# Five gather passes of a graph network get a bound on the index, and the ring of rows is cleared once

## The reference, cut to what matters

```python
edge_index = jnp.stack([src, dst])
h = relu(layernorm(x)); x = x + L0(h)  # attention: q[src] . k[dst], softmax over dst, sum of v[src]
h = relu(layernorm(x)); x = x + L1(h)  # gated unit: mean of h[src] by dst, and mean of h[dst] by src
h = relu(layernorm(x)); x = x + L2(h)  # relations: sum of hW[edge_type, src] by dst, over the degree
h = relu(layernorm(x)); x = x + L3(h)  # attention with LeakyReLU scores, softmax over dst, batch norm
```

## Time and profile before

| what | value |
|---|---|
| time, median of three | 8359.04 us (8329.57 to 8359.52) |
| span of the profiled execution, first to last instruction | 7751.3 us |
| the profiled execution's own time | not recorded; the median lies 607.7 us above the span |
| PE busy | 6251.2 us (81%) |
| DVE busy | 4997.1 us (64%) |
| POOL busy | 4545.2 us (59%) |
| ACT busy | 1562.8 us (20%) |
| mean granted TensorE clock | 0.822 |
| DMA, software queue (POOL's) | 242400 packets, 709.04 MB |
| DMA, hardware queue (SP's) | 187350 packets, 275.48 MB |

### The profile page before, as it was taken

The page is one execution under the profiler, slowest core; times in us unless marked ns, Lnnn a source line. Parts: engine busy times, 40 slices in busy tenths (PEclk is TensorE's granted clock), DMA queues, the critical chain, the costliest instruction groups (busy, mean ns, idle before and its releaser), DMA issues. The chain is left out here.

```text
span 7751.3 us, 82773 instructions
## 1 busy us (share of the span) xinstructions
PE 6251.2 (81%) x23966; PEld 3661.9 (47%) x23966; DVE 4997.1 (64%) x11031; ACT 1562.8 (20%) x3423; POOL 4545.2 (59%) x4618
## 2 busy tenths in 40 slices
PE   8699999996477777888888899888888778878783
PEld 4366666664233333444444444433333355555552
DVE  7799999998666666444444444444444577777777
ACT  5222222222000000000000255200000133333331
POOL 1155555553677777777777311377777356666660
PEclk9799999998765666798988899855555789999997
DMA  2266666666433333544444544433333544444453
GB/s 91 75 177 177 177 176 177 176 177 166 122 99 97 97 98 99 116 132 131 132 128 132 136 164 164 140 101 102 101 101 101 127 130 115 116 115 116 117 107 101
DMA packets 430184, 989.81 MB, mean 128 GB/s; under 512 B 120243, under 2 KB 203377, under 8 KB 423094
## 3 DMA queue, kind: packets, MB, share of 16 engines
q0 software_dynamic: 242400, 709.04, 34.6%
q1 hardware_dynamic: 187350, 275.48, 10.8%
HBM read 851.94 MB, written 132.00 MB: 127 GB/s over the span
## 5 line engine op out<-in xcount | busy, mean ns | idle before, releaser
L876 PE MATMUL psum<-rows,oh 128*128 128x257 f32 (+1 forms) x5280 | 2444.9, 577 | 657.0 <-DMA rows<-h_tab,src_i 201.9
L876 PEld LDWEIGHTS psum<-rows,oh 128*128 128x128 f32 x5280 | 1172.6, 264 | 1879.0 <-issue 1092.2
L885 DVE TENSOR_TENSOR acc<-acc,psum 128x257 f32 (+1 forms) x1760 | 741.4, 421 | 1110.6 <-PE psum L876 986.1
L799 POOL DMA_INDIRECT rows<-qv_tab,src_i x880 | 845.9, 961 | 848.5 <-PE psum L1060 496.5
L1395 POOL DMA_INDIRECT rows<-xh_tab,src_i x880 | 874.2, 993 | 562.3 <-PE psum L1474 248.6
L818 POOL DMA_INDIRECT rows<-h_tab,src_i x880 | 911.3, 1036 | 290.8 <-issue 244.3
L818 POOL DMA_INDIRECT rows<-hw_tab,rel_i x880 | 875.4, 995 | 283.7 <-issue 267.7
L818 POOL DMA_INDIRECT rows<-h_tab,wts x880 | 875.8, 995 | 268.0 <-issue 247.3
L885 DVE TENSOR_TENSOR kh<-kh,psum 128x257 f32 x880 | 370.8, 421 | 643.2 <-PE psum L876 605.3
L1009 PE MATMUL psum<-kh,oht 128*128 x1760 | 505.3, 400 | 5.6
L1474 PE MATMUL psum<-rows,oh 128*128 128x272 f32 x1184 | 403.4, 458 | 131.5 <-issue 130.2
(11 more groups left out here) (461 smaller groups left out, 9415.5 us busy)
## 6 DMA issues: line engine op xcount, KB each, us to landing
wts<-node_rows SPq DMA_DIRECT2D x220, 256.0 KB
hw_tab<-acc SPq DMA_DIRECT2D x50, 1024.0 KB, 4.1
rows<-part_tab SPq DMA_DIRECT2D x50, 512.0 KB, 5.4
rows<-qv_tab,src_i POOLq DMA_INDIRECT x880, 3.7
rows<-h_tab,src_i POOLq DMA_INDIRECT x880, 2.8
rows<-h_tab,wts POOLq DMA_INDIRECT x880, 2.8
rows<-hw_tab,rel_i POOLq DMA_INDIRECT x880, 2.8
rows<-xh_tab,src_i POOLq DMA_INDIRECT x880, 3.2
```

The costliest lines, as they stand in the source:

```text
L799: nc.gpsimd.indirect_dma_start(rows[:, b, 0:width], None, table, bass.IndirectOffsetOnAxis(index, 0)).then_inc(ring[b], 16)
L876: mm = nc.tensor.matmul(slot_bank(n, plan), oh[:, n % RING // GROUP, n % GROUP], row, start=True, stop=True)
L885: nc.vector.tensor_tensor(to, to, slot_bank(n, plan), ALU.add).then_inc(acc_done, 1)
```

## The change

All five passes issue their gathers through a new helper `rows_at`, with a bound on the index: N - 1 = 6249, in L2 N times 8 - 1 = 49999. An index above it is no error; its row is not fetched, and the place in the ring keeps what it held. So that this is never something undefined, POOL clears the whole ring once, in the `reload` stage behind the sort, in which it had nothing to do. The number of gathers, their waits and their counters stay as they were.

```diff
+    def reload_gpsimd(pool):
+        nc.gpsimd.memset(flat, 0.0)
+
+    stage_of(sync=reload_sync, gpsimd=reload_gpsimd, vector=reload_vector, tensor=reload_tensor, scalar=reload_scalar)
...
+    def rows_at(to, table, index, known=N):
+
+        return nc.gpsimd.indirect_dma_start(to, None, table, bass.IndirectOffsetOnAxis(index, 0),
+                                            bounds_check=known - 1, oob_is_err=False)
+
     def gather(pool, j, b, table, width, index):
 
         pool.wait_ge(agg_done, prev(j, b, RING))
-        nc.gpsimd.indirect_dma_start(rows[:, b, 0:width], None, table,
-                                     bass.IndirectOffsetOnAxis(index, 0)).then_inc(ring[b], 16)
+        rows_at(rows[:, b, 0:width], table, index).then_inc(ring[b], 16)
...
-    def gather_ahead(pool, m, to, table, index):
+    def gather_ahead(pool, m, to, table, index, known=N):
...
-        nc.gpsimd.indirect_dma_start(to, None, table,
-                                     bass.IndirectOffsetOnAxis(index, 0)).then_inc(row_landed(m)[0], 16)
+        rows_at(to, table, index, known).then_inc(row_landed(m)[0], 16)
...
-                nc.gpsimd.indirect_dma_start(held(n)[:, 0:ACCW], None, xh_tab,
-                                             bass.IndirectOffsetOnAxis(src_i[:, n:n + 1], 0)).then_inc(row_in(n)[0], 16)
+                rows_at(held(n)[:, 0:ACCW], xh_tab, src_i[:, n:n + 1]).then_inc(row_in(n)[0], 16)
...
-            gather_ahead(pool, m, l2_rows[:, m % HELD, 0:D], hw_tab, rel_i[:, n:n + 1])
+            gather_ahead(pool, m, l2_rows[:, m % HELD, 0:D], hw_tab, rel_i[:, n:n + 1], N * RELS)
```

More of the change, by code:

```diff
@@ L723, in reload_scalar @@
             give(act, 16 * (TILES // 2 + 1 - ((TILES - 1 - p) // 3 + 1)), out_a[p])
-    stage_of(sync=reload_sync, vector=reload_vector, tensor=reload_tensor, scalar=reload_scalar)
+    def reload_gpsimd(pool):
+        nc.gpsimd.memset(flat, 0.0)
+    stage_of(sync=reload_sync, gpsimd=reload_gpsimd, vector=reload_vector, tensor=reload_tensor, scalar=reload_scalar)
     TI = TILES // 2
```

## The result

The changed kernel takes 8429.4 us (median of four runs; 8422.0 to 8467.6), the kernel before beside it 8344.3 us. The ratio is 1.0119, 95% interval 1.0096 to 1.0142, so 85 us slower by the medians and 99 by the ratio, where 24 us faster were forecast. The profiled execution took 8431.8 us, its span is 8430.0 us: only 1.8 us lie around the span.

The account below looks back on a forecast made before the run. POOL's descriptor pace was taken to bound L1 and L2 (2640 gathers, 3466 us, 45% of the span). Tails -24 us, bound zero, memset zero: 8359 - 24 = 8335 us; range 8200 to 8740, the forecast's own 8310 to 8360.

Parts of the forecast that it names:

- The bound in each gather: All 4400 gathers of the five passes: the bound costs zero, and skipped rows save zero of POOL's time.
- 5.4 ns for a look-up: Each gathered row: 0.685 us of a gather's 1.25 us taken as looking up the rows' indices.
- rival B: Gathers with skipped rows: they save POOL's work, 114 us in three passes plus 24, giving 8221 us; chance 0.24.
- Rival A: Every gather: POOL tests each row, 0.077 us a gather, 203 us in 2640, giving 8538 us; chance 0.30.
- threshold of 0.025 us for a measurable loss: Gathers of L1 and L2: from 0.025 us more each, the loss is over 42 us and can be measured.
- Pace by spacing, not by duration: L1 and L2: POOL's 1.25 us start to start sets the pace, not the 0.95 us duration; no slack.
- Tails, 24 us: Ends of L1's second pass and L2: unfetched padding rows save 15 and 9 us, together 24 (14 to 30).
- Memset, zero with a cover of 26 us: Reload stage: 7.1 us on POOL hidden beside VectorE's 26 us chain; cost zero, upper end 7 us.
- L0 and L3 hide up to 0.48 and 0.24 us: L0 and L3: POOL's waits of 496.5 and 248.6 us let a gather grow that much before the pass feels it.
- 607.7 us carried over as lying around the span: Whole kernel: timed median 8359.0 us against profiled span 7751.3 us; the difference was carried over unchanged.
- C: Dropped rows: out-of-bounds rows still make a transfer, tails and bytes stay, 8359 us; chance 0.08.

Follow-up runs that it names:

- e14: Kernel before with the bound only on the gathers of L0 and L3; 1.0016 at the quick level (kernel before 7743.9 us).
- e6: Kernel before with the bound only on the 1760 gathers of L0 and L3; 1.0099 at the slow level (kernel before 8324.9 us).
- e11: Kernel before with a never exceeded bound on the gathers of L0 and L3 only; 1.0094 at the slow level.
- e10: Kernel before with the bound only on the 2640 gathers of L1 and L2; 1.0029 at the slow level.
- e13: The changed kernel run again, unaltered, at the quick level; 1.0109 to the kernel before.
- e1: The kernel before, unchanged, profiled and timed again at the quick level; 7752 us, ratio 1.000.
- e16: Kernel before, no bound, with a one-number POOL memset ahead of each of L0's gathers; 1.0002 at the quick level.
- e7: Measuring kernel: bounds dropping different shares of rows in L1's second pass, 128 or 64 rows with and without bound in L2; slow level, no ratio given.
- e3: The changed kernel with each bound value put in a POOL register once, without 4400 register moves; 1.0081 to the kernel before, quick level.
- e2: The changed kernel with a bound that no index exceeds, so every row is fetched; 1.0147 to the kernel before, quick level.
- e5: Kernel before with the ring cleared; register moves meant ahead of each gather were not in the program that ran; 1.0008, slow level.
- e15: Kernel before, no bound, with each padding edge naming a row of its own; 0.9963 at the quick level.
- e4: Kernel before with only the POOL memset that clears the ring added, no bound; 1.0006 at the quick level.
- e12: Kernel before, no bound, with a one-number POOL memset ahead of each of L0's gathers; 1.0177 at the slow level.
- e8: Kernel before, no bound or clearing, with each padding edge naming a row of its own; 0.9998 at the slow level.

## Why the prediction was wrong, step by step

**The step that failed: "The bound in each gather ... I take zero, for the many rows that are in bounds".** It is 0.05 us a gather (1.25 to 1.30), on 2640 gathers that the prediction itself had shown to have no slack; at the quick level these passes hold the loss (e14, with the bound on the other two only, is at 1.0016).

The timed runs of the result were at the slow level. There the same 0.05 us is paid mostly in L0 and L3 (e6 and e11, 0.99 and 0.94%) and less in L1 and L2 (e10, 0.29%), so that there the step "a gather may become up to 0.48 or 0.24 us dearer, roughly, before the pass feels it" failed as well.

At the quick level, e13 against e1 by their profiles (+62.6 us): the passes of L1 and L2 grow by 34, 32 and 15 us, less than 44 each, because some longer spacings became shorter or fewer (over 1.9 us, L2 has 20 and then 1); the tails take 26 away; L0's start is 7 later; L0 grows by 6, L3 is 11 shorter; the rest is 5. L3's 11 us are a difference of the sets: against e16, of e13's own set and with no bound, L1 and L2 grow by 35, 32 and 19 us, L3 by 2, and the spans differ by 77.6 us, as the timed medians do.

Why it was missed: the estimate split the gather into rows, 5.4 ns for a look-up, and asked what a comparison adds to a row. Half the rows save 0.7 ns each (e7), close to the direct load's 0.6 ns a piece, so of the 0.685 us by which a gather exceeds a direct load of 128 pieces nearly all belongs to the instruction and there is no look-up of 5.4 ns. The saving of rival B therefore had nothing behind it. Rival A's mechanism, a test in every gather whether its rows are in bounds or not, is what happened; its 0.077 us came near the 0.05 partly by luck, since 0.6 ns a row is about three times what e7 gives for a row and the fixed part was not in it; its sentence that a fixed cost for an instruction counts in the same way, and its threshold of 0.025 us for a measurable loss, are what held. The register move, which it named as an example of such a fixed cost, is not it (e3). The Trainium skill, GPSIMD Engine Reference, section Elementwise (side-by-side cycle accounting), puts data-dependent branching at about 12 cycles an element, by which the prediction estimated 1.28 us a gather if each row is tested by a branch. 0.05 us was measured, so no such branch is there.

**Pace by spacing, not by duration.** Right at the quick level. A cost inside the duration (0.95 to 1.00) left the 0.30 us beside it as they were, and e2 shows the passes growing. At the slow level the same passes hardly grow (e10: 1269, 1285 and 1250 us against 1278, 1273 and 1246 in e5): a full ring stops POOL anyway, and its stops shrink by most of what its gathers gain, 220 us of long spacings in L2 to 176.

**Tails, 24 us.** Right in mechanism and size, where it can be seen: 20.4 to 4.4 us in L1's second pass, 15.5 to 5.4 in L2 (e1 to e13), 26 us. The reason given, one row read by all descriptors, is shown by e15. The DMA share of the last 24 slots of L2, which the prediction wanted below 0.3, is 0.03 (e13).

**Memset, zero with a cover of 26 us.** Wrong: 6.9 us by the timeline (e4). The cover was VectorE's chain, and VectorE was stopped by the memset. The prediction named this as its upper end.

**L0 and L3 hide up to 0.48 and 0.24 us.** Right at the quick level (e14, e16), wrong at the slow one, where with the bound L0 takes 1684 to 1708 us against 1628 to 1644. The slack was read from POOL's waits. Such a wait says that POOL was ready before its place was free; it doesn't say how long TensorE can do without the row. At the slow level gathers that come later go with more stops of TensorE and a lower clock (e6, e12).

**607.7 us carried over as lying around the span.** Wrong; 1.8 us lie there. The forecast summed differences, so this did not move its value, but the gap was the sign that the profile was of another level than the runs, where the limits differ.

**C** was rightly held to be unlikely: the bytes go as worked out (39.5 of 39.7 MB) and so do the tails. But no packet goes. L2's gathers make 48 packets each, and in e13's last 24 slots, with every row dropped, 23 gathers still show 1087 packets, with 0.01 MB.

**Left open.** What makes TensorE and VectorE fall behind at the slow level: where the trace shows a landing, the row was in place and the engines idle, and the marks that would name what ended their waits are mostly missing ("remote"). How the bound's price divides between instruction and row, beyond two points. That PE's stops cause the lower clock is an agreement over twelve profiles and of two edits that share nothing but POOL's delay; no run changed the clock by itself.

## What to carry to other kernels

Before pricing a change by the row, halve the rows in one measurement: here 93% of an indirect gather's pace belongs to the instruction by that measurement, and a bound that drops rows costs 0.05 us each time and saves none of POOL's time. If padding is a problem because all of it reads one row, give it different rows: at the quick level that took the whole gain (29 us) at no price per gather, at the slow one it gained nothing that could be measured. And compare the profiled execution's own time with the timed runs before anything else; here a gap of 7% meant that the profile showed another regime.

## What was not expected of the hardware

- A gather of 128 rows with a bound takes 1.30 us from start to start, 1.25 without; the same with none, half, 87% or nearly all rows dropped. With 64 rows it is 1.246 against 1.207.
- Dropped rows leave the number of packets as it was (242400 in all), even where a gather drops all of its rows.
- In the last 24 slots gathers whose 128 indices name one row land after 15.8 us (L1's second pass) and 7.6 us (L2), after 2.8 and 3.0 us with a row each, at the same bytes.
- POOL's memset of 8320 columns holds up a VectorE step with SBUF operands for its whole length (0.69 to 7.55 us), but a memset of 8160 columns doesn't hold up one that reads PSUM (0.69 us).
- The same program runs at 7750 or 8320 us for whole sets of runs, and an edit of 0.24 us per waiting gather costs nothing on the one and 1.8% on the other.
- At the slow level a row can lie ready for 18 us (median of the 36 gathers of e8's L2 that show it) before it is summed, while TensorE and VectorE stand for 10 to 20 us at a time.
